# Gate, logits and key bound in the score banks, transposes of the next tokens between them, and the output bias added to the residual on GpSimd

## The reference

```
n = layernorm(x);  Q = n Wq' + bq;  K = ctx Wk' + bk;  V = ctx Wv' + bv      16 heads of 32
per token: score = Q K' over the 16 heads (16 x 16);  attn = softmax(score) V
x1 = x + attn Wo' + bo
z = layernorm(x1);  logits = z gate' (8 experts);  softmax, top 2, combine weights
out = x1 + sum over the 2 chosen experts of w * down(silu(gate) * up) + shared expert(z)
```

## Time and profile before

| | us |
|---|---|
| three runs | 1443.02, 1440.78, 1442.44 (median 1442.44) |
| the profiled execution | 1443.51 |
| its span, first to last instruction | 1441.8 |
| TensorE busy | 1341.0 (93% of the span) |
| VectorE busy | 884.6 (61%) |
| ScalarE busy | 676.2 (47%) |
| GpSimd busy | 372.9 (26%) |

### The profile page before, as it was taken

The page is one execution under the profiler, slowest core; times in us unless marked ns, Lnnn a source line. Parts: engine busy times, 40 slices in busy tenths (PEclk is TensorE's granted clock), DMA queues, the critical chain, the costliest instruction groups (busy, mean ns, idle before and its releaser), DMA issues.

```text
span 1441.8 us, 34233 instructions
## 1 busy us (share of the span) xinstructions
PE 1341.0 (93%) x11411; PEld 1007.7 (70%) x11412; DVE 884.6 (61%) x1952; ACT 676.2 (47%) x1502; POOL 372.9 (26%) x480
## 2 busy tenths in 40 slices
PE   4799899999999997889999999999999999999997
PEld 4688787888888885657676756666666666657675
DVE  6888888888888887767855533323322322324566
ACT  6286767777676666621444523333333333332221
POOL 4322222222222220005576011111111111105554
PEclk9899999999999998899999999999999999999999
DMA  5557766776766757496744522222222222227986
GB/s 198 132 143 189 194 196 187 201 204 201 194 185 188 196 142 261 128 356 128 132 66 73 143 95 81 87 80 80 87 80 80 86 82 80 84 68 238 317 306 227
DMA packets 212740, 223.20 MB, mean 155 GB/s; under 512 B 84693, under 2 KB 142109, under 8 KB 212334
## 3 DMA queue, kind: packets, MB, share of 16 engines
q1 hardware_dynamic: 193608, 178.62, 43.9%
q0 software_dynamic: 12880, 35.47, 8.3%
q10 hardware_dynamic: 6198, 8.40, 1.9%
HBM read 129.30 MB, written 67.96 MB: 137 GB/s over the span
## 4 chain that ended last, share of the span: by engine, by line
PE 77%; DVE 11%; ACT 3%; issue 3%; DMA 3%; SPq 1%; POOL 1%; another core or an unknown queue 0%; DVEq 0%; POOLq 0%; ACTq 0%
PE psum_b L735 42%; PE psum_a L735 29%; PE psum_b L1026 2%; PE psum_b L1048 2%; DVE z_parts L1492 1%; SPq L677 1%; DVE k_scale L1414 1%; PE psum_b L761 1%; DMA zt_in<-z_columns 1%; DVE d_m L1716 1%; DVE wdn L1824 1%; DMA wgu_in<-expert_rows,pos_ix 1%; DVE gate_act L1690 1%; DMA heads<-in_wk_t 1%; ACT z_parts L1130 1%
## 5 line engine op out<-in xcount | busy, mean ns | idle before, releaser
L735 PE MATMUL psum_a<-wgu,zg_t 128*128 x1704 | 267.7, 314 | 2.2 <-DVE zg_t L1835 1.7
L735 PEld LDWEIGHTS psum_a<-wgu,zg_t 128*128 128x128 f16 x1704 | 166.7, 98 | 89.6 <-issue 10.2
L735 PE MATMUL psum_a<-zt_in,wsgu 128*128 128x256 f16 x1536 | 172.6, 275 | 7.7 <-DMA zt_in<-z_columns 5.2
L735 PEld LDWEIGHTS psum_a<-zt_in,wsgu 128*128 128x128 f16 x1536 | 149.9, 98 | 32.6 <-issue 7.5
L2058 POOL DMA_INDIRECT zg<-z_rows,gather_ix x71 | 67.2, 946 | 404.4 <-DVE gather_ix L1831 397.3
L1840 DVE SCALAR_TENSOR_TENSOR silu<-psum_a,w_scale,silu 128x352 f32<-128x352 f32 x71 | 41.5, 584 | 191.2 <-ACT silu L1313 191.2
L735 PE MATMUL psum_b<-wdn,act_t 128*128 (+1 forms) x639 | 149.6, 379 | 1.6 <-DVE act_t L1847 1.6
L1945 POOL TENSOR_SCALAR var_eps<-mv 128x1 f32<-128x1 f32 x64 | 28.2, 440 | 431.7 <-DVE mv L1391 290.1
L1313 ACT ACTIVATE silu<-psum_a,w_scale 128x352 f32<-128x352 f32 x71 | 39.3, 553 | 202.6 <-PE psum_a L735 202.6
L735 PE MATMUL psum_b<-wsdn,sh_t 128*128 128x512 f16 x540 | 122.5, 379 | 6.1 <-DVE sh_t L1697 5.5
L735 PE MATMUL psum_b<-cx_t,wk 128*128 128x256 f32 x768 | 104.8, 295 | 12.6 <-DVE k_scale L1434 6.3
(11 more groups left out here) (256 smaller groups left out, 2363.9 us busy)
## 6 DMA issues: line engine op xcount, KB each, us to landing
expert_rows<-y_sb SPq DMA_DIRECT2D x71, 256.0 KB
k_st<-k_parts SPq DMA_DIRECT2D x192, 64.0 KB, 2.1
q_st<-q_parts SPq DMA_DIRECT2D x180, 64.0 KB, 2.0
wgu_in<-in_wgu_t SPq DMA_DIRECT2D x8, 1408.0 KB, 17.7
x_sb<-in_x SPq DMA_DIRECT2D x16, 512.0 KB, 5.5
cx_in<-in_ctx_t SPq DMA_DIRECT2D x16, 512.0 KB, 8.9
x_res<-in_x SPq DMA_DIRECT2D x16, 512.0 KB, 6.3
value_rows<-heads SPq DMA_DIRECT2D x16, 512.0 KB, 3.4
```

Source lines behind the costliest of these rows:

```text
L735: return nc.tensor.matmul(o, l, r, start=start, stop=stop)
```

## The change

The diff makes these edits.

- Banks: in the passes the gate products (now R) and the turned logits (RT) go to A0, the bank of scores half 0, and M0 to A1, that of half 1. After the last pass the old steps L and LT in B2 are kept.
- TensorE's order: M0 of pass i-1 moves to the next pass, between chunks 0 and 1 of K. `attend(0)`, `attend(1)` come before `route`; `turn_x` of the next pass comes between `route` and `turn_logits`.
- The bias matmul is gone; GpSimd adds bo, replicated over 128 partitions, to the residual x_res, once per pass, and VectorE's `add_attended` waits for that. `split_bias` is gone from VectorE. bo is loaded as 128 rows instead of 3.
- ScalarE turns both halves of z out before the first `z_high`.
- VectorE does `attended_out` before `bound_out`.
- In the last pass the fetch of the values is issued by GpSimd instead of SP, with a semaphore of its own.

```diff
-ROUTE = [("L", "B2")]
-TURN_ROUTE = [("LT", "B2")]
-BOUND = [("M0", "B3")]
+ROUTE = [("R", "A0")]
+LAST_ROUTE = [("L", "B2")]
+TURN_ROUTE = [("RT", "A0")]
+LAST_TURN = [("LT", "B2")]
+BOUND = [("M0", "A1")]
...
-FULL_PASS = (AHEAD + SCORES + AHEAD_KQ + OUT + AHEAD_V + BEHIND + ROUTE
-             + [("P0", "A2"), ("P1", "A3")] + TURN_ROUTE + BOUND)
+FULL_PASS = (AHEAD + SCORES + AHEAD_KQ + OUT + AHEAD_V + BEHIND + [("P0", "A2"), ("P1", "A3")] + ROUTE + LAST_ROUTE
+             + BOUND + TURN_ROUTE + LAST_TURN)
...
+        bo_rep = sb("bo_rep", [P, D], F32, one)
...
# SP
             def body(i, behind, ahead, ahead3, rows_from=None):
-                fetch_values(i)
+                if ahead:
+                    fetch_values(i)
# TensorE
             def turn_logits(i):
-                wait_free(pe, "LT", i)
+                wait_free(pe, turn_step(i), i)
+                settle(pe)
+                wait_drained(pe, route_step(i), i)
                 settle(pe)
...
             def project_out(s, i):
...
-                mm(bank_ap(step), ones3[:, 0:P], bias3[:, :], True, False)
...
                 if ahead:
-                    turn_x(i)
+                    project_k(i, (0,))
+                if not (isinstance(i, int) and i == 0):
+                    turn_bound(i - 1)
                 if ahead:
-                    project_k(i, (0, 1))
+                    project_k(i, (1,))
                 scores(0, i)
...
                 if behind:
                     turn_z(i)
-                if behind:
-                    route(i)
                 attend(0, i)
                 attend(1, i)
                 if behind:
+                    route(i)
+                if ahead_next:
+                    turn_x(i + 1)
+                if behind:
                     turn_logits(i)
-                if ahead:
-                    turn_bound(i)
...
+            turn_x(0)
+            body(0, False, True, True)
             pe.wait_ge(wo_split, 1)
-            pe.wait_ge(bias_ready, 1)
-            with pe.Fori(1, NB - 1) as i:
-                body(i, True, True)
+            with pe.Fori(1, NB - 2) as i:
+                body(i, True, True, True)
+            body(NB - 2, True, True, False)
# ScalarE
             def z_out(i):
                 turned_out(i, 0)
+                turned_out(i, 1)
                 z_high(i, 0)
-                turned_out(i, 1)
...
-            act.dma_start(b_raw, bo.partition_broadcast(3)).then_inc(bias_loaded, 16)
+            act.dma_start(bo_rep[:, :], bo.partition_broadcast(P)).then_inc(bias_loaded, 16)
# VectorE
-            def split_bias():
...
                     wait_full(dve, f"O{s}", i)
-                    dve.wait_ge(res_loaded, i * 16)
+                    dve.wait_ge(res_biased, (i - 1) * SUB + (s + 1))
...
             def body(i, behind, ahead, ahead2, weighs=0):
-                bound_out(i - 1)
                 if behind:
                     attended_out(i)
+                bound_out(i - 1)
# GpSimd
+            def add_bias(i):
+                pool.wait_ge(res_loaded, i * 16)
+                settle(pool)
+                for s in range(SUB):
+                    G.tensor_tensor(x_res[:, s, :], x_res[:, s, :], bo_rep[:, :], ALU.add).then_inc(res_biased, 1)
...
             def body(i, behind, ahead2):
+                if behind:
+                    add_bias(i)
                 if ahead2:
                     for half in range(SUB):
                         inverse_std(half, stat_no(i + 2, 0, half))
...
             body(NB - 2, True, False)
+            fetch_values(NB - 1)
             body(NB - 1, True, False)
+            add_bias(NB)
```

More of the change, by code:

```diff
@@ L77 @@
 BEHIND = [("Z0", "B2"), ("Z1", "B3")]
-ROUTE = [("L", "B2")]
-TURN_ROUTE = [("LT", "B2")]
-BOUND = [("M0", "B3")]
+ROUTE = [("R", "A0")]
[3 more added lines that the diff above has]
+BOUND = [("M0", "A1")]
 SCORES = [(f"S{s}", f"A{s}") for s in range(SUB)]
-FULL_PASS = (AHEAD + SCORES + AHEAD_KQ + OUT + AHEAD_V + BEHIND + ROUTE
-             + [("P0", "A2"), ("P1", "A3")] + TURN_ROUTE + BOUND)
+FULL_PASS = (AHEAD + SCORES + AHEAD_KQ + OUT + AHEAD_V + BEHIND + [("P0", "A2"), ("P1", "A3")] + ROUTE + LAST_ROUTE
+             + BOUND + TURN_ROUTE + LAST_TURN)
 BANK_OF = dict(FULL_PASS)
 IS_AHEAD = {name for name, _ in AHEAD + AHEAD_KQ + AHEAD_V + BOUND}
-IS_BEHIND = {name for name, _ in OUT + BEHIND + ROUTE + TURN_ROUTE}
+IN_PASSES = {name for name, _ in ROUTE + TURN_ROUTE}
+ONLY_LAST = {name for name, _ in LAST_ROUTE + LAST_TURN}
+IS_BEHIND = {name for name, _ in OUT + BEHIND} | IN_PASSES
 def steps_of(i):
     names = [name for name, _ in FULL_PASS]
+    if i == NB:
+        return [n for n in names if n in IS_BEHIND - IN_PASSES | ONLY_LAST]
+    names = [name for name in names if name not in ONLY_LAST]
     if i < 0:
         return [n for n in names if n in IS_AHEAD]
-    if i == NB:
-        return [n for n in names if n in IS_BEHIND]
     return [n for n in names if not (i == 0 and n in IS_BEHIND) and not (i == NB - 1 and n in IS_AHEAD)]
@@ L105, in earlier_fills, with route_step, turn_step @@
         return whole + sum(n in mine for n in names[:names.index(step)])
-    return (i - 1) * len(mine) + earlier_fills(step, 1)
+    return (i - 1) * len(mine - ONLY_LAST) + earlier_fills(step, 1)
+def route_step(i):
+    return "L" if isinstance(i, int) and i == NB else "R"
+def turn_step(i):
+    return "LT" if isinstance(i, int) and i == NB else "RT"
 class Chain:
@@ L187, in build @@
         wgate = sb("wgate", [P, KC, HD], F32, one)
-        bias3 = sb("bias3", [P, D], BF16, one)
-        ones3 = sb("ones3", [P, BT], BF16, one)
+        bo_rep = sb("bo_rep", [P, D], F32, one)
         other = sb("other", [PAIR, PAIR], F32, one)
@@ L828, in attend @@
                 if s == 0:
-                    pe.wait_ge(v_moved, (i + 1) * (GT * 16))
+                    if isinstance(i, int) and i == NB - 1:
+                        pe.wait_ge(v_moved_last, GT * 16)
+                    else:
+                        pe.wait_ge(v_moved, (i + 1) * (GT * 16))
                 elif not (isinstance(i, int) and i == 0):
@@ L845, in project_out @@
                         last = mm(bank_ap(step), at_t[:, ap, kc, s * P:(s + 1) * P], wo[:, wp, kc, :],
-                                  False, kc == KC - 1 and (ap, wp) == PARTS[-1])
+                                  kc == 0 and (ap, wp) == PARTS[0], kc == KC - 1 and (ap, wp) == PARTS[-1])
                 last.then_inc(full[BANK_OF[step]], 1)
@@ L852, in turn_bound, with body @@
                 nc.tensor.transpose(bank_ap("M0")[:, 0:P], c_rep[:, :], ident[:, :]).then_inc(full[BANK_OF["M0"]], 1)
-            def body(i, behind, ahead):
+            def body(i, behind, ahead, ahead_next):
                 if isinstance(i, int) and i == NB - 1:
@@ L953, in shared @@
                 down(i, b)
-            body(NB - 1, True, False)
-            for step in ("S0", "S1"):
+            body(NB - 1, True, False, False)
+            for step in ("RT", "S1"):
                 wait_drained(pe, step, NB - 1)
@@ L1612, in body @@
                     shared_low(3)
+                if behind:
+                    turned_logits_out(i)
+                if isinstance(i, int) and i == NB - 1:
                     find_scale(wsd_scale, psum_b[0][:, P:2 * P])
@@ L1617, in body @@
                     dve.sem_inc(wd_scaled, 1)
-                if behind:
-                    turned_logits_out(i)
             def x_low(i):
@@ L1658, in _ @@
             values_out(-1)
-            split_bias()
             body(0, False, True, True, PIECE)
@@ L1951, in _ @@
             mark(G.memset(wgate[:, :, E:HD], 0.0))
-            mark(G.memset(ones3[:, :], 1.0))
-            link(G.memset(bias3[:, :], 0.0))
+            own_.wait()
             G.affine_select(out=ident[:, :], in_=ident[:, :], compare_op=ALU.not_equal, fill=1.0, base=0,
@@ L1971, in _, with fetch_values @@
             split_context(0)
+            def fetch_values(i):
+                pool.wait_ge(v_stored, (i + 1) * 16)
+                settle(pool)
+                if not (isinstance(i, int) and i == 0):
+                    wait_full(pool, "P1", i - 1)
+                    settle(pool)
+                src = v_d[bass.ds(i * BT, BT), :].rearrange("(n t) (h d) -> t h n d", t=GT, h=H)
+                for t in range(GT):
+                    at = t // PAIR * HD + t % PAIR
+                    pool.dma_start(v_p[at:at + HD - t % PAIR:PAIR, :, :], src[t]).then_inc(v_moved_last, 16)
             def weights_low(n, w, w_in, done):
```

39 lines of the change are left out of this document (13 added, 26 removed).

## The result

The changed kernel takes 1439.3 us (median of 14 runs, 1435.8 to 1442.3), the kernel before 1443.4 in the same set (1440.8 to 1448.8). The ratio is 0.9968, 95% interval 0.9958 to 0.9979: faster, by 4.1 us or 0.3%. I had forecast 17 to 18 us, and the time is 0.3 outside my range. The sign was right, the size wrong by a factor of four.

What follows compares the result with a forecast made beforehand. TensorE bounds the kernel, VectorE's loop only 2.5 us a pass behind and taking over. Gains of 6.2 (start), 2.9 (pass 1), 5.2 (passes 2 to 13) and 3.1 (end) sum to 17.4, giving 1425 us, range 1410 to 1439.

Steps and rivals of the forecast that it cites:

- Start: Before the loop and at the turn to pass 1: 6.1 + 0.8 gained, 0.7 lost to bo's load, 6.2 us in all.
- Pass 1: First pass, VectorE beginning level and TensorE still setting the pace: 31.1 us instead of 34.03, 2.9 less.
- Passes 2 to 13: Steady passes, paced by VectorE and slowed by the cast: 33.6 us each instead of 34.03, 5.2 gained over twelve.
- VectorE's loop: VectorE's own work per pass, 31.5 us, plus 1.3 idle from the new gate wait: 32.8, replacing TensorE as pacesetter.
- the new hole: TensorE's wait before z's transposes, replacing its three holes: about 1.6 us, expected in the profile as 1.5 to 2.5.
- the cast holds z's second half: In each pass VectorE's z half 1 waits for GpSimd's context cast: 0.8 us more, bounds 0 and 3.3.
- The row at 9.14: Before the loop, a normalisation starting at 9.14 beside a cast at 9.41 took 1.58 us; model for the cast collision.
- the two bias matmuls: In O of each pass, TensorE loses two bias matmuls of 0.30 us each, 0.6 off its own time.
- GpSimd's additions: Two 128 x 512 bias additions per pass, about 1.2 us each: taken to cost VectorE 0, bounds 0 and 2.4.
- the key scale has only single operands: VectorE's key scale beside GpSimd's additions would not be held, since it lacks two SBUF operands: cost 0.
- Passes 14, 15 and behind: Last passes and after the loop: 2.0 + 0.5 + 0.6, 3.1 us gained; VectorE no longer late in pass 14.
- rival of a late fetch: Last value fetch comes late on GpSimd's queue: 4 us, 1429; chance 0.15 together with no shorter passes.

Runs made afterwards that it cites:

- second profile: The unmodified changed kernel timed and profiled once more in another set: median 1443.8 us, kernel before 1448.6, ratio 0.9983.
- order_only: Changed kernel with the old bias (split on VectorE, matmul in the output projection), so banks, order and moved value fetch alone: 0.9913 of the kernel before.
- zero_matmuls: Changed kernel with two bf16 matmuls a pass, now adding zeros, put back ahead of the output projection: 0.9927 of the kernel before.
- attend_first: Changed kernel with both attention halves ahead of z's transposes and the next x's transposes ahead of the gate products: 0.9931 of the kernel before.
- half_first: Changed kernel with GpSimd's context conversion after VectorE's z and the first attention half ahead of z's transposes: 0.9865 of the kernel before.
- bias_only: Kernel before with the bias part alone: GpSimd adds it to the residual, no split, no bias matmul, old banks and order: 0.9939 of the kernel before.
- fetch_on_sp: Changed kernel with the last value fetch back on SP's queue: 0.9958 of the kernel before.
- bias_after_scale: Changed kernel where GpSimd adds the bias in passes 1 to 15 only after VectorE has written the key scale: 0.9997 of the kernel before.
- cast_later: Changed kernel where GpSimd converts the context of two blocks on only after VectorE has written this pass's z: 0.9896 of the kernel before.
- joined: half_first plus ScalarE issuing the shared weight loads before the last pass and the last bias additions after shared_low: 0.9861 of the kernel before.
- last_bias_later: Changed kernel where GpSimd adds the bias for the last block only when shared_low is done: 0.9970 of the kernel before.
- transition: Changed kernel where ScalarE issues the three shared weight loads at pass 15's start and the last bias additions follow shared_low: 0.9966 of the kernel before.
- weights_early: Changed kernel where GpSimd, not SP, issues the three shared weight loads, ahead of its last value fetch: 0.9975 of the kernel before.
- half_first_bias: half_first with GpSimd's bias addition also held until after the key scale: 0.9866 of the kernel before.
- order_cast: order_only with GpSimd's context conversion moved after VectorE's z: 0.9904 of the kernel before.

## Why the prediction was right in sign and wrong in size

**Start: forecast 6.2, measured 7.6** (6.9 in the second profile). Right, with its mechanism: K half 2 of pass 0 starts at 53.42 with no wait, where it waited 6.30, and VectorE's low part of it at 60.55, where it was at 66.71. order_only, which keeps the split, starts pass 1 4 to 5 us later; each half of the diff alone gives 3 us here.

**Pass 1: forecast 31.1, 2.9 less.** From K step to K step it takes 31.5 in one profile, near the forecast, and 33.6 in the other (34.1 before). In the second the clock fell at 82.5 us; by the granted clock that is 1.7 of the 2.1 between them.

**Passes 2 to 13: forecast 33.6 each, measured 33.82 in both profiles** (33.64 is the mean with pass 1). So they gave 2.5 us in place of 5.2; the length of a pass is nearly right, the mechanism only in half. VectorE's loop took over, the new hole stands before z (forecast 1.5 to 2.5, measured 1.25 + 0.61), and the cast holds z's second half for 0.63 (forecast 0.8, largest duration 1.17 against 1.3). The section cited from the Trainium skill (SBUF — State Buffer, "Who interferes with whom"), by which the first to issue wins, fits: the cast starts at 304.16, z's second half at 304.3, and GpSimd went through undisturbed at 1.04. The row at 9.14 fits it less well: there VectorE's operation is recorded as starting before the cast and was held all the same. Without a fall of the clock these passes take 33.1 on average (33.3 in the second profile), less than forecast, and with one 34.8. The clock stands nowhere in my sum. That the forecast of a pass came so near is in part luck: VectorE's loop was 0.3 to 0.5 too long in it, and the clock, left out, was worth 0.5 to 0.7. I counted the two bias matmuls among TensorE's savings and, rightly, as worth nothing where VectorE sets the pace. I did not ask what an idle TensorE costs. order_only, zero_matmuls, attend_first and half_first show it from four sides: work kept, added or moved in the hole, and the clock stays up, but for one pass of zero_matmuls. The kernel before shows as much idle time in a pass, spread over three holes, at no cost in clock.

**GpSimd's additions: forecast 0 a pass, bounds 0 and 2.4.** Their length is right (1.26 each, forecast 1.2). They cost VectorE 0.22 a pass on the key bias in the changed kernel, up to 0.76 where passes are faster. The step from "the key scale has only single operands" to no cost failed at one instruction: the 128 x 4 operation with its scalar operand per partition was held.

**Passes 14, 15 and behind: forecast +3.1, measured -5.8, and about -2 more behind.** This is the step that failed, the largest miss of the sum. I wrote that VectorE "isn't late any more" in pass 14 "and TensorE keeps the gain of a pass: 2.0", and I took the transfers there as given. VectorE is late there. Its low parts of pass 14's keys, and SP's moves of them, in the changed kernel and then before:

```profile
524.76 1.29 DVE L1405 TENSOR_TENSOR k_parts<-heads,k_parts 128x512 f16<-128x512 f32 x2
526.14 9.10 SPq L503 DMA_DIRECT2D k_st<-k_parts  x12
...
534.33 1.31 DVE L1402 TENSOR_TENSOR k_parts<-heads,k_parts 128x512 f16<-128x512 f32 x2
535.73 7.69 SPq L494 DMA_DIRECT2D k_st<-k_parts  x12
```

Counted from pass 14's first K step (512.51 and 525.25), the low parts start at 12.3 in place of 9.1 and the moves at 13.6 in place of 10.5. TensorE, ahead of VectorE at the K step, has lost that lead again at the first scores of pass 15 (32.1 and 32.3), and VectorE starts z of pass 15 at 50.6 in both. Of the forecast 2.0 only 0.2 came. The two kernels without the new order need 66.2 and 66.7 from pass 14 to `gate_up`, all with it 69.9 to 75.3, the variants with fixes included. The weights are issued 34.5 us after pass 14's first K step where it was 31.4: in SP's queue they stand behind the moves of keys and queries, back to back from 526 to 543, which begin 3.1 late with VectorE's low parts of the keys (12.9 or more after the K step at the end of the first, in every kernel with the new order; 9.8 before and in bias_only). Beside the moved value fetch they then take 3 to 4 us longer to land, and ScalarE waits 4.50 for them. Then comes what they hold up: the second half of `shared_low` starts 3.7 later against the K step than before (64.0 and 60.3), and loses 2.0 more beside the additions, which makes the 5.8. In `gate_up`, counted in the next piece, half clock costs 2.3. My rival of a late fetch had the right place but the wrong victim: the fetch on GpSimd's queue wasn't late itself, it made the weights late. No variant takes the loss away, so how much of the 5.8 can be had back, and by which edit, stays open.

**To the end.** The piece behind `gate_up` takes 850.3 to 855.7 us over all profiles but that of fetch_on_sp (870.5), with code that is nearly the same from there. Of the first profile's 5.4, 2.3 is the half clock named above, and 2.5 the wait at 1403, which the second profile hasn't. There is only one profile of the kernel before, so how typical its 850.3 is stays open.

## What to carry over

When another engine sets the pace, work saved on TensorE is not neutral: here it lengthened a hole, and behind that hole the granted clock fell in some passes, for more than the saving. Look in the windows view at the clock behind each wait that a change creates, and fill the hole with work that is ready. Price the last passes of a pipelined stage apart from the steady ones, transfers first: ask which engine is behind when they begin, and what stands ahead of each load in its queue and beside it on the DMA engines. And test the halves of a joined change alone; here one of them was faster than both together, and the other no slower.

## What the runs showed of the hardware

- In ten profiles (the changed kernel twice, bias_after_scale, cast_later, fetch_on_sp, joined, last_bias_later, transition, weights_early, zero_matmuls) the granted clock fell to 0.50 for some 3 us at a time in 37 of the 120 passes 2 to 13. In each of the 37 TensorE had waited 1.6 to 2.5 us ahead of z, both waits of a pass together. There was no fall in the 12 passes each of order_only (1.2 to 1.4 together), half_first (0.3 to 1.5), half_first_bias (0.5 to 1.6) and attend_first (no wait for z), nor before and in bias_only, with 2.3 a pass in three holes. order_cast has one such fall behind a wait of only 1.02. And 2.4 brought no fall in pass 3 of the changed kernel where 1.8 did in pass 10; what tells them apart the runs don't show.
- Behind 5.2 to 7.3 us of idle before `gate_up`, its first 48 products took 6.9 to 8.1 us in the fifteen profiles with the new order, behind 2.55 (bias_only) 7.07, behind 1.71 (before) 5.40. From 584 to 587 the granted clock of the changed kernel was 0.50.
- VectorE's normalisation of 128 x 512 with two per-partition scalars took 0.54 alone and 1.17 beside GpSimd's cast. A 128 x 4 operation with one took 0.23 alone and, where GpSimd's addition of 128 x 512 stood beside it, up to 0.99 on average over seven passes (attend_first). 128 x 1 operations started beside the same addition were not held (0.15 to 0.21).
- Beside the 2.8 MB load of the shared weights the last four 64 KB moves of pass 14's queries took 6.5 to 7.1 us from issue to landing (transition) and 7.8 to 10.2 (weights_early), where they took 2.0 to 2.1 in the changed kernel. Beside the eight 64 KB moves of the values, a 1280 KB load took 14.9 us in place of 11.7.
